# A Householder step whose norm and products come out of the strip matmuls, the masked column made by VectorE

## The chip, the cores and the metric

One NeuronCore of a Trainium2 chip runs the whole program. The metric is device time in microseconds, the median of three runs: 6160.08 us before the change (6158.68 to 6161.56).

## The reference, cut to what matters

A first layer (graph products and four small LSTMs, with a residual layer norm) is followed by a spectral graph layer that needs all eigenvectors of a 512 x 512 matrix:

```python
d_inv_sqrt = jnp.where(deg > 0, jax.lax.rsqrt(deg), 0.0)
L_norm = d_inv_sqrt[:, None] * (jnp.diag(deg) - A) * d_inv_sqrt[None, :]
_, U = jnp.linalg.eigh(L_norm)
agg = jnp.einsum('mn,bnd->bmd', U.T, features)
h = jax.nn.relu(agg @ W1 + b1)
out = jnp.einsum('nm,bmd->bnd', U, h @ W2 + b2)
```

## The kernel before

The eigenvectors come from a Householder tridiagonalization (510 steps), leaves of 16 by QR sweeps, divide and conquer, and a back transformation. The change touches the first of these. The matrix `lap` lies in four tiles of 128 rows; step k works on the T = 4 - (k+1)//128 tiles that are left, so 127, 128, 128 and 127 steps have T = 4, 3, 2, 1. The trailing matrix is updated only every 16 steps (`NB`): in between, the vectors v and w of each step go into the panel `pan`, which stands beside `lap` in `lapw`, four copies side by side so that every strip of columns has one. j = k % 16 is the place in the panel.

One step runs like this. TensorE multiplies column k (`acols`) with strips of `lapw` (L487), four strips of 32 output partitions per tile, and so gets the product with the matrix and the panel's coefficients at once; L491 fetches the panel's row k+1. While the strips run, VectorE takes the root that ScalarE made (L307), forms the pivot `pair`, the Householder vector `v` (L919) and two reciprocals (L911 to L921). When y is there it picks and reduces it (L924 to L934), builds the next column's old part `a1` (L932, L938) and the product for v'y (L940). It waits for the gate (L942), makes `pcol`, `tau_row` and the pieces of the next column, and the product for L499 (L958). L961 gives the next column `acols`; then come its norm's products (L886, L887), and with L499's sum the vector w (L966, L969), which goes into the panel. Four ones-matmuls per step carry sums over the partitions to all of them: the norm (L470), the gate (L495, prepared by GpSimd's L219 to L232), v'y (L497) and v'p (L499). ScalarE copies v and w into `swap` and `pan` (L310, L318, L319) and scales `pcol` (L321).

Each engine takes its instructions in the order written. Between them stand semaphores; `put` and `after` are VectorE's own, `link` is one with a wait at once.

## Time and profile before

| | us |
|---|---|
| median of the runs | 6160.08 |
| profiled execution | 6150.05 |
| its span | 6147.9 |
| VectorE busy | 4304.7 |
| TensorE matmul busy | 3290.3 |
| ScalarE busy | 932.4 |
| GpSimd busy | 790.6 |

The page's chain that ended last is VectorE in 53% and TensorE in 37% of the span; no engine is busy all the time. Busy shares are means over stages that differ: the steps of the change fill one stretch, and what an edit in them is worth is read from the order of time of one step.

### The profile page before, as it was taken

The numbers are of one execution on the slowest core, as the hardware profiler recorded it, in microseconds if no ns is written. First come the engines' busy times: TensorE is split into PE (matmuls) and PEld (weight loads), VectorE is DVE, ScalarE is ACT, GpSimd is POOL, SyncE is SP. The second block draws the span as 40 slices with busy tenths as digits, with TensorE's granted clock in tenths as the row PEclk, the third lists the DMA queues.
The fourth block names the chain that finished last, engine by engine and source line by source line (L and its number), as shares of the span: only waits on it lengthen the run. The fifth ranks groups of instructions, "written<-read, shape, count | busy, mean of one in ns | idle before, by whom it ended". The sixth has DMA issues, their size and how long they took to land.

```text
span 6147.9 us, 78861 instructions
## 1 busy us (share of the span) xinstructions
PE 3290.3 (54%) x19000; PEld 2342.0 (38%) x19000; DVE 4304.7 (70%) x27212; ACT 932.4 (15%) x4314; POOL 790.6 (13%) x3424
## 2 busy tenths in 40 slices
PE   7877738888888888777777730000002212230476
PEld 4333226565566666666666630000002212120243
DVE  1222286666677777888888889999968888889534
ACT  2432201111122222222222210000000000000000
POOL 0000001111111111111100014444430000000000
PEclk9988855555555555555555555555555555565578
DMA  2000000000000000000000000000000000000000
GB/s 55 0 0 0 0 0 1 1 1 1 1 1 1 1 1 1 1 1 1 1 1 1 1 1 1 1 1 1 1 1 0 0 0 0 0 0 0 0 0 27
DMA packets 20805, 17.38 MB, mean 3 GB/s; under 512 B 6544, under 2 KB 16784, under 8 KB 20368
## 3 DMA queue, kind: packets, MB, share of 16 engines
q1 hardware_dynamic: 20368, 12.65, 0.8%
q8 instruction: 141, 2.31, 0.2%
q14 instruction: 296, 2.42, 0.1%
HBM read 8.41 MB, written 4.20 MB: 2 GB/s over the span
## 4 chain that ended last, share of the span: by engine, by line
DVE 53%; PE 37%; issue 6%; ACT 2%; SPq 1%; POOL 0%; DMA 0%; DVEq 0%; ACTq 0%; POOLq 0%
PE bank L487 9%; PE bank L436 5%; PE bank L499 5%; PE bank L491 3%; DVE qp L1193 2%; PE bank L470 2%; PE bank L438 2%; DVE ycol L934 2%; DVE dif L1546 2%; PE bank L482 2%; DVE ts L966 1%; DVE qp L1183 1%; DVE tau_row L950 1%; DVE jcol L958 1%; DVE gated L948 1%
## 5 line engine op out<-in xcount | busy, mean ns | idle before, releaser
L487 PE MATMUL bank<-lapw,hid 128*32 128x160 f32 (+3 forms) x10200 | 660.3, 421 | 61.2 <-DVE lapw L907 17.8
L524 PE MATMUL bank<-diag,blk 128*128 128x32 f32 (+1 forms) x96 | 23.3, 416 | 1041.4 <-DVE diag L1310 1030.0
L487 PEld LDWEIGHTS bank<-lapw,hid 128*32 128x32 f32 x10200 | 395.1, 163 | 190.7 <-DVE lapw L969 83.0
L499 PE MATMUL bank<-xp,ones 128*128 128x1 f32 x1020 | 298.9, 362 | 277.9 <-DVE xp L958 277.9
L524 PEld LDWEIGHTS bank<-diag,blk 128*128 128x128 f32 x96 | 21.4, 327 | 1043.5 <-DVE diag L1310 1031.9
L219 POOL TENSOR_TENSOR sq<-hid,ltm 128x4 f32<-128x4 f32 (+3 forms) x510 | 101.0, 198 | 2324.3 <-DVE hid L961 2265.7
L497 PE MATMUL bank<-xp,ones 128*128 128x1 f32 x1020 | 299.0, 362 | 185.4 <-DVE xp L940 185.4
L436 PE MATMUL bank<-hid,onehot 128*128 x504 | 328.2, 769 | 120.0 <-DVE ga L736 67.2
L499 PEld LDWEIGHTS bank<-xp,ones 128*128 128x128 f32 x1020 | 255.3, 311 | 321.6 <-DVE xp L958 321.6
L497 PEld LDWEIGHTS bank<-xp,ones 128*128 128x128 f32 x1020 | 255.3, 311 | 229.1 <-DVE xp L940 229.1
L470 PE MATMUL bank<-xn,ones 128*128 128x2 f32 x1020 | 299.3, 363 | 18.5 <-DVE xn L887 17.6
L491 PEld LDWEIGHTS bank<-lapw,ident 128*128 128x128 f32 x956 | 240.3, 313 | 157.7 <-issue 157.7
L491 PE MATMUL bank<-lapw,ident 128*128 128x2 f32 (+1 forms) x956 | 292.0, 385 | 0.0
L495 PE MATMUL bank<-xn,ones 128*128 128x1 f32 x1020 | 289.1, 353 | 0.0
L495 PEld LDWEIGHTS bank<-xn,ones 128*128 128x128 f32 x1020 | 277.6, 332 | 10.6 <-issue 10.6
L318 ACT ACTIVATE swap<-vcols 128x4 f32<-128x4 f32 (+3 forms) x510 | 105.5, 207 | 1149.4 <-DVE xp L940 1149.4
L470 PEld LDWEIGHTS bank<-xn,ones 128*128 128x128 f32 x1020 | 255.4, 311 | 44.0 <-DVE xn L887 20.8
L924 DVE TENSOR_TENSOR yz<-bank,pick 128x128 f32<-128x128 f32 (+3 forms) x510 | 117.5, 230 | 205.5 <-PE bank L487 205.3
L239 POOL TENSOR_SCALAR zt<-lz,rot 32x32 f32<-32x32 f32 x540 | 194.8, 361 | 474.7 <-DVE rot L1240 425.2
L524 PE MATMUL bank<-wide,ones 128*128 128x128 f32 x80 | 18.3, 402 | 365.7 <-DVE wide L1310 365.7
L436 PEld LDWEIGHTS bank<-hid,onehot 128*128 128x128 f32 x504 | 108.7, 223 | 260.6 <-issue 252.3
L966 DVE TENSOR_SCALAR ts<-bank,tau_row 128x1 f32<-128x1 f32 x510 | 141.3, 277 | 65.1 <-PE bank L499 1.3
(729 smaller groups left out, 8493.1 us busy)
## 6 DMA issues: line engine op xcount, KB each, us to landing
out_x<-xs SPq DMA_DIRECT2D x16, 256.0 KB, 3.3
lapw<-in_adj SPq DMA_DIRECT2D x1, 1024.0 KB, 5.9
bias_rows<-in_L_gnn_bg SPq DMA_DIRECT2D x8, 64.0 KB, 5.6
hid<-lz SPq DMA_DIRECT2D x32, 1.0 KB, 1.7
bias_rows<-in_L_gnn_b SPq DMA_DIRECT2D x4, 64.0 KB, 5.7
wg<-in_L_gnn_Wg SPq DMA_DIRECT2D x2, 64.0 KB, 11.0
wg<-in_L_gnn_W SPq DMA_DIRECT2D x2, 64.0 KB, 3.6
xs<-in_x SPq DMA_DIRECT2D x1, 0.5 KB, 19.7
```

The costliest lines, as they stand in the source:

```text
L239: pool.tensor_scalar(zt[:, 0:2, :], lz[:, i:i + 2, :], rot[:, h, 0, i:i + 1], None, ALU.mult)
L436: m = pe.matmul(bank[4 * h + q][:, 0:cols_], wih_t[:, p - 1, q * P:(q + 1) * P], xt, start=True, stop=(t == 0))
L438: m = pe.matmul(bank[4 * h + q][:, 0:cols_], whh_t[:, p - 1, q * P:(q + 1) * P], state[:, h, 0:cols_], start=False, stop=True)
L470: pe.matmul(bank[0][:, 0:2], ones[:, 0:P], xn[:, 0:2], start=True, stop=True).then_inc(norm_ps, 1)
L482: pe.matmul(bank[4 + t][:, c0:], panx[:, 0, t * P:(t + 1) * P], panx[:, 1, c0:], start=True, stop=True).then_inc(update_ps, 1)
L487: m = pe.matmul(bank[1][32 * q:32 * q + 32, 0:(T + 1) * 32].rearrange("p (u i) -> p u i", i=32), acols[:, t, k:k + 1].to_broadcast([P, 32] ...
L491: pe.matmul(bank[2][:, 0:2 * j], unit(k), lapw[:, t0, N:N + 2 * j], start=True, stop=True).then_inc(rowz_ps, 1)
L495: pe.matmul(bank[4][:, 0:1], ones[:, 0:P], xn[:, 2:3], start=True, stop=True).then_inc(tail_ps, 1)
L497: pe.matmul(bank[3][:, 0:1], ones[:, 0:P], xp[:, 0:1], start=True, stop=True).then_inc(vy_ps, 1)
L499: pe.matmul(bank[2][:, 4 * NB:4 * NB + 1], ones[:, 0:P], xp[:, 1:2], start=True, stop=True).then_inc(vp_ps, 1)
L934: y = put(V.tensor_reduce(ycol[:, t0:], yz[:, t0:, 0:32 + 2 * j], AX.X, ALU.add))
L966: a = put(V.tensor_scalar(ts[:, 6:7], bank[2][:, 4 * NB:4 * NB + 1], tau_row[:, k:k + 1], tau_row[:, k:k + 1], ALU.mult, ALU.mult))
```

## The change

The step is rewritten. GpSimd writes the unit vector of row k+1 into the panel's column 2j (four copies), VectorE writes column k, masked below row k+1, into column 2j+1 (`masked`, four copies). The strips' product then holds, beside y, the pivot element and the squared norm, which VectorE copies into `al`. ScalarE takes the root, GpSimd makes five coefficients of one column, and VectorE the weights from them. y is formed with the column itself instead of v, and v is never formed in the loop; one ones-matmul of three columns (`xd`) gives all sums. The next column is `acols[k+1]`, then w for the panel, then the next masked column. The columns now lie in `vcols`, and v's pivot is added to them behind the loop, where the diagonals are put together differently too.

```diff
-        acols, gate_row = mix, vrow
+        acols = vcols
...
@@ -212,24 +213,25 @@
 
             linked = 0
             for k in range(STEPS):
...
+                t0, j = (k + 1) // P, k % NB
+                T = NT - t0
+                if k == 0:
+                    pool.wait_ge(a_ready, 1)
                 else:
...
+                    pool.wait_ge(y_done, k)
+                if j == 0 and k:
+                    pool.wait_ge(panx_ps, k // NB)
+                pool.tensor_copy(pan[:, t0:, :, j, 0], onehot[:, t0:, k + 1].unsqueeze(2).to_broadcast([P, T, 4])).then_inc(unit_ready, 1)
+                pool.wait_ge(al_ready, k + 1)
+                pool.tensor_scalar(coef[:, 0:1], al[:, 0:1], 0.0, 0.5, ALU.is_ge, ALU.subtract).then_inc(coef_ready, 1)
+                pool.tensor_scalar(coef[:, 1:2], al[:, 0:1], al[:, 0:1], al[:, 1:2], ALU.mult, ALU.add).then_inc(coef_link, 1)
+                pool.wait_ge(coef_link, linked + 1)
+                pool.wait_ge(coef_ready, 3 * k + 1)
+                pool.tensor_tensor(coef[:, 2:3], coef[:, 1:2], coef[:, 0:1], ALU.mult).then_inc(coef_ready, 1)
+                pool.tensor_scalar(coef[:, 3:4], al[:, 1:2], 1e-24, 1e37, ALU.is_le, ALU.mult).then_inc(coef_link, 1)
+                linked += 2
+                pool.wait_ge(coef_link, linked)
+                pool.tensor_tensor(coef[:, 4:5], coef[:, 3:4], coef[:, 1:2], ALU.add).then_inc(coef_ready, 1)
...
@@ -302,27 +304,28 @@
 
             for k in range(STEPS):
                 t0, j = (k + 1) // P, k % NB
...
                 if j == 0 and k:
                     act.wait_ge(panx_ps, k // NB)
                     act.activation(panx[:, 0, t0 * P:], bank[1][0:2 * NB, t0 * P:], ACT.Copy)
                     act.activation(panx[:, 1, t0 * P:], bank[2][0:2 * NB, t0 * P:], ACT.Copy).then_inc(panx_sb, 1)
                     act.wait_ge(updated, k // NB)
+                if k == 0:
+                    act.wait_ge(a_ready, 1)
                 act.activation(tz[:, t0:, 0], lap[:, t0:, k + 1], ACT.Copy).then_inc(edge_ready, 1)
...
+                act.wait_ge(am_ready, k + 1)
+                act.activation(swap[:, t0:, j, 0], pan[:, t0:, 0, j, 1], ACT.Copy).then_inc(v2_ready, 1)
+                act.wait_ge(al_ready, k + 1)
+                act.activation(root[:, 0:1], al[:, 0:1], ACT.Sqrt, scale=al[:, 0:1], bias=al[:, 1:2]).then_inc(norm_root, 1)
+                act.wait_ge(norm_root, 2 * k + 1)
+                act.wait_ge(coef_ready, 3 * k + 1)
+                act.activation(root[:, 1:2], coef[:, 0:1], ACT.Copy, scale=root[:, 0:1]).then_inc(norm_root, 1)
+                act.wait_ge(p_ready, 2 * k + 2)
+                act.activation(w0[:, t0:], pcol[:, t0:], ACT.Copy, scale=th[:, 0:1]).then_inc(w0_ready, 1)
+                act.activation(p_row[:, k:k + 1], wts[:, 0:1], ACT.Copy)
+                act.activation(tau_row[:, k:k + 1], th[:, 0:1], ACT.Copy)
+                act.wait_ge(w_ready, k + 1)
+                act.activation(swap[:, t0:, j, 1], pan[:, t0:, 0, j, 0], ACT.Copy).then_inc(w2_ready, 1)
+                act.activation(ends_row[:, k, :], bank[3][:, 0:3:2], ACT.Copy).then_inc(vy_saved, 1)
             act.activation(tz[:, NT - 1:, 0], lap[:, NT - 1:, N - 1], ACT.Copy).then_inc(edge_ready, 1)
 
             for w in range(SWEEPS):
                 t0, j = (k + 1) // P, k % NB
                 T, c0 = NT - t0, t0 * P
-                pe.wait_ge(norm_in, 2 * (k + 1))
-                pe.matmul(bank[0][:, 0:2], ones[:, 0:P], xn[:, 0:2], start=True, stop=True).then_inc(norm_ps, 1)
                 if k:
                     pe.wait_ge(w_ready, k)
-                    pe.wait_ge(v2_ready, k)
                 if j == 0 and k:
                     pe.wait_ge(w2_ready, k)
+                    pe.wait_ge(v2_ready, k)
...
                     pe.wait_ge(updated, k // NB)
+                pe.wait_ge(a_ready, k + 1)
+                pe.wait_ge(am_ready, k + 1)
+                pe.wait_ge(unit_ready, k + 1)
                 for t in range(t0, NT):
                     strips = lapw[:, t, c0:].rearrange("p (u q i) -> p u q i", q=4, i=32)
                     for q in range(4):
@@ -491,15 +495,10 @@
                     pe.matmul(bank[2][:, 0:2 * j], unit(k), lapw[:, t0, N:N + 2 * j], start=True, stop=True).then_inc(rowz_ps, 1)
                 if k:
                     pe.wait_ge(vy_saved, k)
-                pe.wait_ge(tail_in, k + 1)
-                pe.matmul(bank[4][:, 0:1], ones[:, 0:P], xn[:, 2:3], start=True, stop=True).then_inc(tail_ps, 1)
-                pe.wait_ge(x_ready, k + 1)
-                pe.matmul(bank[3][:, 0:1], ones[:, 0:P], xp[:, 0:1], start=True, stop=True).then_inc(vy_ps, 1)
-                pe.wait_ge(x2_ready, k + 1)
-                pe.matmul(bank[2][:, 4 * NB:4 * NB + 1], ones[:, 0:P], xp[:, 1:2], start=True, stop=True).then_inc(vp_ps, 1)
+                pe.wait_ge(x_ready, 2 * k + 2)
+                pe.matmul(bank[3][:, 0:3], ones[:, 0:P], xd[:], start=True, stop=True).then_inc(vy_ps, 1)
             j = STEPS % NB
             pe.wait_ge(w_ready, STEPS)
-            pe.wait_ge(v2_ready, STEPS)
             pe.matmul(bank[2][:, 0:2 * j], unit(STEPS), lapw[:, NT - 1, N:N + 2 * j], start=True, stop=True).then_inc(rowz_ps, 1)
             pe.wait_ge(diag_in, 1)
             for t in range(NT):
...
             V.memset(swap[:], 0.0)
-            V.memset(pair[:], 0.0)
-            link(V.memset(scrow[:], 0.0))
+            V.memset(p_row[:], 0.0)
+            V.memset(wts[:, 1:2], 2.0)
+            link(V.memset(wts[:, 3:4], 1.0))
...
@@ -874,22 +874,21 @@
             def after(at):
                 dve.wait_ge(tri_link, at)
 
-            bcol_ = pole_gap
-            V.tensor_copy(bcol_[:, :, 0], lap[:, :, 0])
+            V.tensor_tensor(c4[:, 8:9], lap[:, 0, 0:1], ident[:, 0:1], ALU.mult)
             V.tensor_tensor(acols[:, :, 0], lap[:, :, 0], ltm[:, :, 0], ALU.mult).then_inc(a_ready, 1)
-
-            def norms(k):
-
-                t0, e = (k + 1) // P, (k + 1) % P
-                a = acols[:, t0:, k]
-                dve.wait_ge(a_ready, k + 1)
-                V.tensor_tensor(xn[:, 1:2], acols[:, t0, k:k + 1], ident[:, e:e + 1], ALU.mult).then_inc(norm_in, 1)
-                V.tensor_tensor_reduce(jcol[:, 0, t0:], a, a, 1.0, 1e-32, ALU.mult, ALU.add, xn[:, 0:1]).then_inc(norm_in, 1)
-
-            norms(0)
             adds = 0
             rowz = 0
 
+            def masked(k):
+
+                t0 = (k + 1) // P
+                shape = [P, NT - t0, 4]
+                dve.wait_ge(a_ready, k + 1)
+                V.tensor_tensor(pan[:, t0:, :, k % NB, 1], acols[:, t0:, k].unsqueeze(2).to_broadcast(shape), ltm[:, t0:, k + 1].unsqueeze(2).to_broadcast(shape),
+                                ALU.mult).then_inc(am_ready, 1)
...
@@ -898,102 +897,110 @@
 
             for k in range(STEPS):
                 t0, j = (k + 1) // P, k % NB
...
+                T, c0, e = NT - t0, t0 * P, (k + 1) % P
+                a_, here = acols[:, t0:, k], T * 32 + 2 * j
                 if j == 0 and k:
                     for t in range(t0, NT):
                         adds += 1
                         dve.wait_ge(update_ps, adds)
                         m = V.tensor_tensor(lap[:, t, c0:], lap[:, t, c0:], bank[4 + t][:, c0:], ALU.add)
                     m.then_inc(updated, 1)
...
+                    masked(k)
 
                 dve.wait_ge(y_done, k + 1)
+                V.tensor_scalar(al[:], bank[1][:, here:here + 2], 1e-36, None, ALU.add).then_inc(al_ready, 1)
                 a = put(V.tensor_tensor(yz[:, t0:, 0:32], bank[1][:, 0:T * 32].rearrange("p (t i) -> p t i", i=32),
                                         pick[:].unsqueeze(1).to_broadcast([P, T, 32]), ALU.mult))
                 if j:
                     dve.wait_ge(w2_ready, k)
...
                     a = put(V.tensor_tensor(yz[:, t0:, 32:32 + 2 * j], panel_cols(j, t0), panel_rows(bank[1][:, T * 32:T * 32 + 32], j, T), ALU.mult))
+                after(a)
+                y = put(V.tensor_reduce(ya[:, t0:, 1], yz[:, t0:, 0:32 + 2 * j], AX.X, ALU.add))
+                dve.wait_ge(edge_ready, k + 1)
+                if j:
                     rowz += 1
                     dve.wait_ge(rowz_ps, rowz)
...
+                    after(put(V.tensor_tensor(tz[:, t0:, 1:1 + 2 * j], panel_cols(j, t0), panel_rows(bank[2], j, T), ALU.mult)))
+                a1done = put(V.tensor_reduce(ya[:, t0:, 0], tz[:, t0:, 0:1 + 2 * j], AX.X, ALU.add))
+                after(y)
+                V.tensor_tensor_reduce(jcol[:, 0, t0:], a_, ya[:, t0:, 1], 1.0, 0.0, ALU.mult, ALU.add, xd[:, 2:3]).then_inc(x_ready, 1)
+                dve.wait_ge(norm_root, 2 * k + 1)
+                r = put(V.reciprocal(ts[:, 0:1], root[:, 0:1]))
                 after(a1done)
+                V.tensor_tensor(xd[:, 0:2], ya[:, t0, :], ident[:, e:e + 1].to_broadcast([P, 2]), ALU.mult).then_inc(x_ready, 1)
+                dve.wait_ge(norm_root, 2 * k + 2)
+                dve.wait_ge(coef_ready, 3 * k + 2)
+                after(r)
+                p = put(V.tensor_scalar(wts[:, 0:1], ts[:, 0:1], coef[:, 2:3], root[:, 1:2], ALU.mult, ALU.add))
+                dve.wait_ge(coef_ready, 3 * k + 3)
+                c = put(V.reciprocal(cn_row[:, k:k + 1], coef[:, 4:5]))
+                after(p)
+                q = put(V.tensor_scalar(ts[:, 1:2], al[:, 0:1], wts[:, 0:1], coef[:, 4:5], ALU.mult, ALU.add))
+                m = put(V.tensor_tensor(yam[:, t0:, :], ya[:, t0:, :], ltm[:, t0:, k + 1].unsqueeze(2).to_broadcast([P, T, 2]), ALU.mult))
+                after(c)
+                g = put(V.tensor_tensor(wts[:, 2:5:2], wts[:, 0:1].to_broadcast([P, 2]), cn_row[:, k:k + 1].to_broadcast([P, 2]), ALU.mult))
+                after(q)
+                V.reciprocal(th[:, 0:1], ts[:, 1:2]).then_inc(p_ready, 1)
+                after(m)
                 if k:
                     dve.wait_ge(w0_ready, k)
...
+                V.scalar_tensor_tensor(pcol[:, t0:], yam[:, t0:, 0], wts[:, 0:1], yam[:, t0:, 1], ALU.mult, ALU.add).then_inc(p_ready, 1)
+                dve.wait_ge(p_ready, 2 * k + 1)
+                h = put(V.tensor_scalar(th[:, 1:2], th[:, 0:1], th[:, 0:1], wts[:, 0:1], ALU.mult, ALU.mult))
+                dve.wait_ge(p_ready, 2 * k + 2)
                 after(g)
...
+                b = put(V.scalar_tensor_tensor(nbcol[:, t0:], pcol[:, t0:], wts[:, 4:5], yam[:, t0:, 0], ALU.mult, ALU.subtract))
                 dve.wait_ge(vy_ps, k + 1)
...
+                V.tensor_tensor_reduce(jcol[:, 1, 0:2], bank[3][:, 1:3], wts[:, 3:5], 1.0, 0.0, ALU.mult, ALU.add, zy[:, 0:1])
+                z = put(V.tensor_tensor_reduce(jcol[:, 2, 0:3], bank[3][:, 0:3], wts[:, 0:3], 0.5, 0.0, ALU.mult, ALU.add, zy[:, 1:2]))
+                after(max(z, h, b))
+                x = put(V.tensor_tensor(xk[:], zy[:], th[:], ALU.mult))
+                after(x)
+                am = pan[:, t0:, 0, j, 1]
+                V.scalar_tensor_tensor(acols[:, t0:, k + 1], am, xk[:, 0:1], nbcol[:, t0:], ALU.mult, ALU.subtract).then_inc(a_ready, 1)
                 dve.wait_ge(w0_ready, k + 1)
...
+                V.scalar_tensor_tensor(pan[:, t0:, :, j, 0], am.unsqueeze(2).to_broadcast([P, T, 4]), xk[:, 1:2], w0[:, t0:].unsqueeze(2).to_broadcast([P, T, 4]),
                                        ALU.mult, ALU.subtract).then_inc(w_ready, 1)
+                if k + 1 < STEPS and (k + 1) % NB:
+                    masked(k + 1)
 
             j = STEPS % NB
             dve.wait_ge(rowz_ps, rowz + 1)
             dve.wait_ge(w2_ready, STEPS)
             dve.wait_ge(edge_ready, STEPS + 1)
             after(put(V.tensor_tensor(tz[:, NT - 1:, 1:1 + 2 * j], panel_cols(j, NT - 1), panel_rows(bank[2], j, 1), ALU.mult)))
...
+            after(put(V.tensor_reduce(ya[:, NT - 1, 0:1], tz[:, NT - 1, 0:1 + 2 * j], AX.X, ALU.add)))
+            V.tensor_tensor(c4[:, 9:10], ya[:, NT - 1, 0:1], ident[:, P - 1:P], ALU.mult)
             dve.wait_ge(a_ready, STEPS + 1)
             for t in range(NT):
...
                 lo = 1 if t == 0 else 0
                 m = V.tensor_tensor_reduce(tail[:, t * P:(t + 1) * P - lo], acols[:, t, t * P - 1 + lo:(t + 1) * P - 1], ident[:, lo:], 1.0, 0.0, ALU.mult, ALU.add, c4[:, 4 + t:5 + t])
             after(put(m))
...
+            V.memset(diag[:], 0.0)
+            for t in range(NT):
                 m = V.tensor_scalar(wide[:, t, :], ident[:], c4[:, 4 + t:5 + t], None, ALU.mult)
...
+            after(put(m))
+            V.tensor_copy(diag[:, 0, 0:1], c4[:, 8:9])
+            V.tensor_copy(diag[:, NT - 1, P - 1:P], c4[:, 9:10]).then_inc(diag_in, 1)
             dve.wait_ge(vy_saved, STEPS)
...
+            use, live_ = slice(0, STEPS), junk[:, 0:STEPS]
+            after(put(V.tensor_scalar(live_, cn_row[:, use], 1e-30, None, ALU.is_gt)))
+            after(put(V.tensor_tensor(vrow[:, use], cn_row[:, use], ends_row[:, use, 1], ALU.mult)))
             dve.wait_ge(diag_ps, 1)
             link(V.tensor_copy(diag_row[:], bank[0][:]))
             link(V.tensor_copy(off_row[:, 0:N - 1], bank[1][:, 1:N]))
...
+            link(V.tensor_tensor(tail[:, use], off_row[:, use], live_, ALU.mult))
+            link(V.tensor_tensor(off_row[:, use], off_row[:, use], tail[:, use], ALU.subtract))
+            link(V.tensor_tensor(tail[:, use], p_row[:, use], live_, ALU.mult))
+            link(V.tensor_tensor(off_row[:, use], off_row[:, use], tail[:, use], ALU.subtract))
+            link(V.tensor_scalar(live_, live_, -1.0, 1.0, ALU.mult, ALU.add))
+            link(V.tensor_tensor(tail[:, use], ends_row[:, use, 0], live_, ALU.mult))
+            link(V.tensor_tensor(diag_row[:, 1:STEPS + 1], vrow[:, use], tail[:, use], ALU.add))
+            for t in range(NT):
+                lo = 1 if t == 0 else 0
+                band = slice(t * P - 1 + lo, (t + 1) * P - 1)
+                link(V.tensor_tensor(tail[:, t * P:(t + 1) * P - lo], ident[:, lo:], p_row[:, band], ALU.mult))
+                link(V.tensor_tensor(vcols[:, t, band], vcols[:, t, band], tail[:, t * P:(t + 1) * P - lo], ALU.add))
```

## Rows read from the trace of the kernel before

**Rows 1.** Stretch table, the 510 steps: length, busy PE, PEld, DVE, ACT, POOL, clock.

```profile
889.60:3608.00 2718.40, 2149.24 (x15537) 1682.82 (x15537) 2026.60 (x15307) 608.76 (x3630) 349.56 (x1785) 0.50 0.01 1
```

**Rows 2.** Order of time, one step, three tiles: start, duration, engine, line, tiles.

```profile
2407.87 1.05 PEld L487 LDWEIGHTS bank<-lapw,hid 128*32 128x32 f32 x24 [0.18 <-DVE lapw L969]
...
2409.31 0.60 PE L491 MATMUL bank<-lapw,ident 128*128 128x12 f32 x2
2409.45 0.26 DVE L924 TENSOR_TENSOR yz<-bank,pick 128x96 f32<-128x96 f32 x1 [0.37 <-PE bank L487]
...
2411.37 0.22 DVE L957 SCALAR_TENSOR_TENSOR ats<-hid,scrow,ltm 128x3 f32<-128x3 f32 x1
2411.51 0.15 DVE L958 CUSTOM_DVE_ANT_0 jcol<-vcols,pcol 128x3 f32<-128x3 f32 x1
...
2411.63 0.23 DVE L961 SCALAR_TENSOR_TENSOR hid<-ats,bank,bm 128x3 f32<-128x3 f32 x1
...
2411.73 0.59 PE L499 MATMUL bank<-xp,ones 128*128 128x1 f32 x2 [0.54 <-DVE xp L958]
...
2411.96 0.18 DVE L886 TENSOR_TENSOR xn<-hid,ident 128x1 f32<-128x1 f32 x1
...
2412.35 0.28 DVE L966 TENSOR_SCALAR ts<-bank,tau_row 128x1 f32<-128x1 f32 x1
...
2412.66 0.24 DVE L969 SCALAR_TENSOR_TENSOR lapw<-vcols,ts,w 128x12 f32<-128x12 f32 x1
...
2412.96 1.05 PEld L487 LDWEIGHTS bank<-lapw,hid 128*32 128x32 f32 x24 [0.18 <-DVE lapw L969]
```

**Rows 3.** The same view, four tiles left.

```profile
895.35 1.80 PEld L487 LDWEIGHTS bank<-lapw,hid 128*32 128x32 f32 x32 [0.18 <-DVE lapw L969]
...
897.78 0.29 DVE L924 TENSOR_TENSOR yz<-bank,pick 128x128 f32<-128x128 f32 x1 [1.22 <-PE bank L487]
...
901.27 1.80 PEld L487 LDWEIGHTS bank<-lapw,hid 128*32 128x32 f32 x32 [0.18 <-DVE lapw L969]
```

**Rows 4.** The same view, two tiles left.

```profile
2851.53 0.52 PEld L487 LDWEIGHTS bank<-lapw,hid 128*32 128x32 f32 x16 [0.18 <-DVE lapw L969]
...
2855.88 0.52 PEld L487 LDWEIGHTS bank<-lapw,hid 128*32 128x32 f32 x16 [0.18 <-DVE lapw L969]
...
2856.68 0.50 PEld L491 LDWEIGHTS bank<-lapw,ident 128*128 128x128 f32 x2 [0.28 <-issue]
...
2857.01 0.21 DVE L924 TENSOR_TENSOR yz<-bank,pick 128x64 f32<-128x64 f32 x1
```

**Rows 5.** The same view, one tile left.

```profile
3562.54 0.20 PEld L487 LDWEIGHTS bank<-lapw,hid 128*32 128x32 f32 x8 [0.18 <-DVE lapw L969]
...
3562.91 0.50 PEld L491 LDWEIGHTS bank<-lapw,ident 128*128 128x128 f32 x2 [0.17 <-issue]
...
3563.66 0.17 DVE L924 TENSOR_TENSOR yz<-bank,pick 128x32 f32<-128x32 f32 x1
...
3566.72 0.20 PEld L487 LDWEIGHTS bank<-lapw,hid 128*32 128x32 f32 x8 [0.18 <-DVE lapw L969]
```

**Rows 6.** Groups by line: count, busy us, mean ns, idle time before them.

```profile
L239 POOL TENSOR_SCALAR zt<-lz,rot 32x32 f32<-32x32 f32 x540 | 194.8, 361 | 474.7 <-DVE rot L1240 425.2
...
L321 ACT ACTIVATE w<-pcol,tau_row 128x4 f32<-128x4 f32 (+3 forms) x510 | 150.9, 296 | 114.6 <-DVE tau_row L950 114.6
...
L232 POOL TENSOR_TENSOR xn<-sq 128x1 f32<-128x1 f32 x383 | 74.9, 195 | 30.0
...
L1087 DVE TENSOR_SCALAR lq<-lq 32x1 f32<-32x1 f32 x36 | 8.7, 242 | 0.0
```

**Rows 7.** Order of time again, start of a panel's transposes, four tiles.

```profile
986.75 0.20 ACT L310 ACTIVATE swap<-lapw 128x4 f32<-128x4 f32 x1
987.07 0.10 PEld L477 LDWEIGHTS bank<-ident,lapw 128*32 128x32 f32 x1 [0.51 <-DVE lapw L969]
```

**Rows 8.** Order of time, a wide link behind the last step.

```profile
3618.95 0.69 DVE L994 TENSOR_TENSOR junk<-pair,vrow 128x510 f32<-128x510 f32 x1
```

102 lines of the change are left out of this document (8 added, 94 removed).

## The prediction

> **What bounds the kernel now.** I read the stretch table first: the 510 Householder steps that the change rewrites fill 889.6 to 3608 us, 2718.4 of the 6147.9 us span, with TensorE at clock 0.50, its 1.2 GHz level, all the time [rows 1]. Nothing outside is touched but a short stretch behind it. Then the order of time of one step with three tiles left (T = 3) [rows 2]. It repeats every 2412.96 - 2407.87 = 5.09 us: the strip products of `lapw` take 1.58 us until VectorE starts `yz`, then VectorE works almost without a gap from 2409.45 to its product for the last ones-matmul (L958), that matmul ends at 2412.32, and two more VectorE instructions (to 2412.90) release the next strips. So a step is a loop of latencies: strips, VectorE's chain, one small matmul, VectorE again. With four tiles the loop is 901.27 - 895.35 = 5.92 us, 2.43 of it strips [rows 3]. With two it is 4.35 and with one 4.18 [rows 4, 5]. There the strips are done sooner (0.94 and 0.51 us: start of the small matmul behind them plus the 0.14 seen in rows 2), but `yz` starts only 1.12 us after them with one tile (3563.66 - 3562.54): the root and the vector `v` are still being made on VectorE. This hidden chain ends last only for T = 2 and 1.
>
> **What the change removes.** Three of the four ones-matmuls per step, with their round trips; one stays. The norm now comes out of the strips themselves: column 2j of the panel holds the unit vector, column 2j+1 the masked column, so `bank[1]` delivers alpha and the squared norm together with y. The chain that made `v` before `yz` goes, which for T = 1 uncovers 1.12 - 0.51 = 0.61 us and for T = 2, where `yz` starts 1.13 after the strips [rows 4], 0.19 us. What comes instead stands behind the strips: root, coefficients and weights can only start after them.
>
> **How I price a VectorE chain.** From rows 2: an instruction that waits for nothing starts its predecessor's duration less 0.08 after it (L957 0.22, L958 0.14 later); one that needs a result starts 0.04 after that ends (L957 to L961, L966 to L969). One that stands behind two waits, the second being the late one, starts 0.10 after (L961 ends 2411.86, L886 at 2411.96). Work on a few columns costs 0.15 (L958) to 0.18 (L886), I take 0.16; with one per-partition scalar 0.22 (L957). With two it costs 0.24 on 32 partitions [rows 6] and 0.28 with an operand from PSUM (L966); I take 0.25 for the three in SBUF.
>
> **The new step, T = 3, j = 6, from the moment y is there.** `al` 0.00; `yz` 0.07; its panel part 0.24 to 0.43; reduction 0.47 to 0.75; `tz` product 0.67 to 0.86 (the row product in `bank[2]` is there by 0.50, L491 starts 0.14 before `yz` and lasts 0.60); second reduction 0.90 to 1.09; the products for `xd` 1.01 to 1.33, a reciprocal between them; `wts` 1.35 to 1.60 (behind a third wait, 0.10). Then the reciprocal of `coef[4]`, which comes from GpSimd (below), `ts[1]` 1.67 to 1.92, `yam` 1.84, `g` 1.92, `th` 2.00 to 2.17, `pcol` 2.08 to 2.30, `h` 2.22 to 2.47, `nbcol` 2.39 to 2.61, the two `zy` sums 2.53 to 2.77, `xk` 2.81 to 2.97, new column 3.01 to 3.24, `w` for the panel 3.16 to 3.40, masked column 3.32 to 3.49. The one matmul (1.33 + 0.05 + 0.60 + 0.03 = 2.01) is hidden behind this. ScalarE's root and its product (0.15 + 0.03 + 0.38, then 0.05 + 0.29; 0.29 is L321 with one operand as scale [rows 6], the root has a second, for which I add 0.09) end at 0.90 and are hidden too.
>
> **The masked column.** It is a 128 x 4T product, about 0.17 us by L958's and L886's size, and it is the last thing that the strips wait for: they need `w_ready`, `a_ready`, `am_ready` and `unit_ready`, four waits where there were two. It starts 0.16 after `w` and so adds 0.09 to the chain. Between VectorE and TensorE one late wait costs 0.06 (L969 to L487 [rows 2]); with three awaited, the late one second, 0.12 (ScalarE ends 986.95, TensorE starts 987.07 [rows 7]). Four I put at 0.145, bounds 0.06 and 0.20. Behind these waits in TensorE's queue stands the whole step. The unit columns come from GpSimd, which is free for them after about 1.6 us; hidden by 1.8 us of slack. In 31 steps (every sixteenth) it goes behind the update of `lapw` instead; there it is not in front of the panel's transposes but in front of the strips all the same, so these steps pay about what the others pay.
>
> **GpSimd's chain.** Five one-column instructions: two with immediates, one with two pointer scalars, two tensor products. The product costs 0.195, the tensor-scalar form 0.361 with one pointer and 32 elements [rows 6], and the dependent product starts 0.08 after its producer (L232's idle 30.0 us by 383). No row shows the one-column forms. Bounds: each as a product, 0.20, or as the row, 0.33 and 0.45 for two pointers. I take 0.22 and 0.38, nearer the product, as 32 elements are part of the 0.361. From `al` at 0.15: 0.08 + 0.19 + 0.38 + 0.08 + 0.165 + 0.22 + 0.08 + 0.195 + 0.05 = 1.44, ready at 1.59. VectorE could take it at 1.52 for T = 3 and at 1.30 for T = 1, so from T = 3 down it sets the time, by 0.03 to 0.25 us.
>
> **The sum.** Chain 3.49 + 0.145 + strips 1.58 = 5.21 for T = 3, against 5.09: +0.12. By the same steps T = 4 (j = 1): 6.06 against 5.92, +0.14. T = 2: 3.63 + 0.94 = 4.57 against 4.35, +0.22; T = 1: 3.63 + 0.51 = 4.14 against 4.18, -0.04. There are 127, 128, 128 and 127 such steps: 17.8 + 15.4 + 28.2 - 5.1 = +56 us. The same bookkeeping gives the old step some 0.02 more than its rows show; I take off 510 x 0.02 = 10. Behind the steps: wide links 0.72 each [rows 8], seven where three were, and eight of 128 columns at about 0.32, less eight of 128 columns at about 0.2: +4. Together +50 on a profiled execution of 6150.05 us, which lies 10 us under the median of the runs, 6160.08. Forecast: 6210 us.
>
> **Rivals.** *GpSimd is dear* (0.16): its tensor-scalar forms cost 0.33 and 0.45, the coefficients are ready at 1.88, and each step grows by 0.3 to 0.5, with one tile by 0.2: over the j by average +179, less the 10, plus the 4, 6333 us (6260 to 6345). For it: the only row of that form, 0.361. Against: its 32 elements and its pointer. The Trainium skill's GPSIMD Engine Reference, section Engine selection, says to leave elementwise work to VectorE, GpSimd being some two times slower for two inputs; here the one-column product is 0.195 against VectorE's 0.15 to 0.18, so the trace shows less, but the hops of 0.08 come on top, and five instructions in a row are where that rule would bite.
>
> *Faster* (0.28): the hand-overs cost what single waits cost, 0.06 before the strips and 0.04 before `wts`, and GpSimd's forms cost 0.20. Then the GpSimd chain is ready at 1.37 and hidden for T = 4 to 2, and the steps are: first the cheap GpSimd, 5 us over before by the average over j; less 510 x 0.09 = 46; less 255 x 0.06 = 15; less the 10; plus 4: -62, 6100 us. It decides if the strips start under 0.08 after the masked column and `coef` is there before VectorE asks. T = 1 gains 0.3 to 0.4 per step in it, which is where the old hidden chain is uncovered [rows 5]. Half of it (one of the two cheap) gives 6140.
>
> *Nothing measurable* (0.12): the pieces cancel, within 12 us, about 0.2%, which is what a measurement of this kernel can tell from no change. The change doing something other than it says isn't open: the masked column is made by VectorE, and ScalarE's copy of `v` (L319) goes; in the kernel before GpSimd made no such column, so what is timed is the whole new step.
>
> *Shared reads*, inside the forecast's range: L886 took 0.18 while a GpSimd product ran beside it, L958 0.15 [rows 2]. The Trainium skill (SBUF — State Buffer, Who interferes with whom) says that a VectorE instruction with two SBUF inputs contends with a GpSimd instruction that reads SBUF. Four such fall beside GpSimd's new chain; at 0.02 each that would be +20 to +40 us, 6240 us.
>
> **How the numbers follow.** Forecast 6210 (6175 to 6255, the bounds of the waits before the strips and half of those of GpSimd's forms), 0.44; dear GpSimd 0.16; faster 0.28; same 0.12. Slower by over 0.2%: 0.60. The range leaves about one in ten on each side: 6110 to 6300.
>
> **What would show it.** In the new profile: T = 3 steps of 5.2 us between strips, T = 1 of 4.1; masked column 0.17 and the strips 0.14 behind its end; idle VectorE time before the reciprocal of `coef`, released by GpSimd, growing from T = 3 to T = 1; no idle time released by the one matmul or by the root. I am wrong if that idle time is missing, if GpSimd's tensor-scalar takes 0.3 or more, or if T = 2 comes out under 4.35.

## The result and the profile after

The changed kernel takes 6290.24 us (median of 4 runs, 6286.64 to 6292.10) against 6159.38 for the kernel before on the same chip: 1.0213 times as long, 95% interval 1.0195 to 1.0231, +131 us. The forecast was 6210, +50. The sign was right, but the loss is more than twice the forecast's: the time lies outside the 6175 to 6255 that were given with it, inside the outer bounds of 6110 to 6300, and within the 6260 to 6345 of the rival *dear GpSimd*. The profiled execution took 6289.45 us, with a span of 6287.7 us.

Two parts of its page, busy time and the chain that ended last:

```profile
PE 2491.2 (40%) x15940; PEld 1659.8 (26%) x15940; DVE 3972.7 (63%) x25687; ACT 1179.3 (19%) x5334; POOL 1117.7 (18%) x4699
DVE 51%; PE 29%; issue 10%; POOL 8%; ACT 2%; SPq 1%; DVEq 0%; DMA 0%; ACTq 0%; POOLq 0%
```

The stretch of the 510 steps, as in [rows 1] (length, busy PE, PEld, DVE, ACT, POOL, clock):

```profile
892.67:3743.77 2851.10, 1347.70 (x12480) 997.92 (x12480) 1690.77 (x13768) 854.15 (x4646) 676.33 (x3061) 0.50 0.00 1
```

It is 2851.1 us long where it was 2718.4: +132.7. The span grew by 139.8, of which 3.1 lies ahead of the steps and 4.0 behind them. Nearly all that is to be explained is in the steps, and the clock is the same. TensorE is busy 802 us less and VectorE 336 us less, and yet the stretch is longer. So busy time was not what set it.

The step that answers to [rows 2] (three tiles, step 246, j = 6), in order of time:

```profile
2488.43 0.16 DVE L911 TENSOR_SCALAR al<-bank 128x2 f32<-128x2 f32 x1 [1.82 <-PE bank L491]
...
2488.68 0.23 POOL L226 TENSOR_SCALAR coef<-al 128x1 f32<-128x1 f32 x1 [3.80 <-DVE al L911]
...
2488.89 0.35 POOL L227 TENSOR_SCALAR coef<-al 128x1 f32<-128x1 f32 x1
...
2489.32 0.19 POOL L230 TENSOR_TENSOR coef<-coef 128x1 f32<-128x1 f32 x1
...
2489.59 0.23 POOL L231 TENSOR_SCALAR coef<-al 128x1 f32<-128x1 f32 x1
...
2489.79 0.27 DVE L934 TENSOR_SCALAR wts<-ts,coef,root 128x1 f32<-128x1 f32 x1
...
2489.91 0.19 POOL L234 TENSOR_TENSOR coef<-coef 128x1 f32<-128x1 f32 x1
...
2490.14 0.16 DVE L936 RECIPROCAL cn_row<-coef 128x1 f32<-128x1 f32 x1
...
2491.52 0.23 DVE L960 SCALAR_TENSOR_TENSOR vcols<-lapw,xk,nbcol 128x3 f32<-128x3 f32 x1
2491.66 0.23 DVE L962 SCALAR_TENSOR_TENSOR lapw<-lapw,xk,w 128x12 f32<-128x12 f32 x1
2491.80 0.17 DVE L887 TENSOR_TENSOR lapw<-vcols,ltm 128x12 f32<-128x12 f32 x1
...
2492.20 1.08 PEld L491 LDWEIGHTS bank<-lapw,vcols 128*32 128x32 f32 x24 [1.87 <-DVE lapw L962]
2492.23 1.51 PE L491 MATMUL bank<-lapw,vcols 128*32 128x128 f32 x24 [1.81 <-DVE lapw L887]
...
2493.80 0.16 DVE L911 TENSOR_SCALAR al<-bank 128x2 f32<-128x2 f32 x1 [1.82 <-PE bank L491]
```

Two places stand out. The reciprocal L936 starts 0.03 behind the end of GpSimd's last sum L234 (2490.105 to 2490.139). The masked column ends at 2491.97, the strips' weights load starts at 2492.20 and their first product at 2492.23, 0.26 behind it. In [rows 2] the same passage took 0.06 (L969 ends 2412.90, L487 starts 2412.96).

The same steps as in [rows 3 to 5] in the changed kernel, four tiles, then two, then one:

```profile
901.42 0.16 DVE L911 TENSOR_SCALAR al<-bank 128x2 f32<-128x2 f32 x1 [2.67 <-PE bank L491]
```

```profile
2966.49 0.16 DVE L911 TENSOR_SCALAR al<-bank 128x2 f32<-128x2 f32 x1 [1.18 <-PE bank L491]
...
2968.21 0.16 DVE L936 RECIPROCAL cn_row<-coef 128x1 f32<-128x1 f32 x1 [0.20 <-POOL coef L234]
...
2971.21 0.16 DVE L911 TENSOR_SCALAR al<-bank 128x2 f32<-128x2 f32 x1 [1.18 <-PE bank L491]
```

```profile
3699.00 0.16 DVE L911 TENSOR_SCALAR al<-bank 128x2 f32<-128x2 f32 x1 [0.76 <-PE bank L491]
...
3700.71 0.16 DVE L936 RECIPROCAL cn_row<-coef 128x1 f32<-128x1 f32 x1 [0.22 <-POOL coef L234]
...
3703.27 0.16 DVE L911 TENSOR_SCALAR al<-bank 128x2 f32<-128x2 f32 x1 [0.76 <-PE bank L491]
```

Step by step (the next `al` after the first of these is at 907.66):

| tiles | before | forecast | measured | over the forecast |
|---|---|---|---|---|
| 4 | 5.92 | 6.06 | 6.24 | 0.18 |
| 3 | 5.09 | 5.21 | 5.37 | 0.16 |
| 2 | 4.35 | 4.57 | 4.72 | 0.15 |
| 1 | 4.18 | 4.14 | 4.27 | 0.13 |

The excess changes by 0.05 only while the strips shrink from 2.4 to 0.5 us. Most of it sits in a fixed part of the step, not in the strips or the panel.

Groups by line, the new small ones, as [rows 6]:

```profile
L227 POOL TENSOR_SCALAR coef<-al 128x1 f32<-128x1 f32 x510 | 177.1, 347 | 0.0
L934 DVE TENSOR_SCALAR wts<-ts,coef,root 128x1 f32<-128x1 f32 x510 | 139.3, 273 | 47.0 <-POOL coef L230 8.6 <-POOL coef L234 0.9 <-DVE ts L928 0.6
...
L226 POOL TENSOR_SCALAR coef<-al 128x1 f32<-128x1 f32 x510 | 118.6, 233 | 1935.4 <-DVE al L911 1935.4
...
L887 DVE TENSOR_TENSOR lapw<-vcols,ltm 128x16 f32<-128x16 f32 (+3 forms) x510 | 86.5, 170 | 0.0
L936 DVE RECIPROCAL cn_row<-coef 128x1 f32<-128x1 f32 x510 | 82.8, 162 | 56.4 <-POOL coef L234 39.6
```

And what one line of TensorE's queue left, the wait for the masked column (count, ns):

```profile
L486 PEldq EVENT_SEMAPHORE  x509: 51/51/51, 898.8 to 3741.2; - x170
```

The durations came out as priced: 0.23 and 0.35 for GpSimd's forms (0.22 and 0.38 forecast), 0.170 for the masked column (0.17). The last row is the clue to the passage. Of TensorE's four waits ahead of the strips, the one written first in the code (for `w`) rides on the load; the others are two instructions of their own in front of it. In step 246 the trace has the one for the masked column, written third, at 2492.015, 0.04 behind its end, the other (for the column, written second, and the unit, written fourth, both long fulfilled) at 2492.126, and the load at 2492.202. So the records do not keep the written order, except that the first rides on the load.

So two theories: **A**, the late wait stands as an instruction of its own with another behind it, and that costs 0.08 to 0.17 us a step; **C**, GpSimd's chain holds VectorE's reciprocal (the recorded texts of the runs on GpSimd's chain call this their Theory A). Their rival: VectorE's own order sets the step and both only seem late.

### The profile page after: what moved, and what is told of

Read it like the earlier page. It is cut to its first block, busy times and chain, and to the rows that moved or that the text cites. A ratio compares the mean times of both kernels' runs of the same rounds, so it can differ in the third digit from the quotient of the medians.

```text
span 6287.7 us, 73604 instructions
## 1 busy us (share of the span) xinstructions
PE 2491.2 (40%) x15940; PEld 1659.8 (26%) x15940; DVE 3972.7 (63%) x25687; ACT 1179.3 (19%) x5334; POOL 1117.7 (18%) x4699
## 4 chain that ended last, share of the span: by engine, by line
DVE 51%; PE 29%; issue 10%; POOL 8%; ACT 2%; SPq 1%; DVEq 0%; DMA 0%; ACTq 0%; POOLq 0%
PE bank L491 11%; PE bank L439 5%; POOL coef L227 2%; PE bank L441 2%; DVE qp L1200 2%; DVE vcols L960 2%; DVE dif L1553 2%; DVE nbcol L952 2%; PE bank L483 2%; DVE ts L938 2%; POOL coef L231 1%; POOL coef L226 1%; DVE xk L957 1%; DVE al L911 1%; DVE qp L1190 1%
## 5 line engine op out<-in xcount | busy, mean ns | idle before, releaser
L491 PE MATMUL bank<-lapw,vcols 128*32 128x160 f32 (+3 forms) x10200 | 659.8, 419 | 934.4 <-DVE lapw L887 922.0
L491 PEld LDWEIGHTS bank<-lapw,vcols 128*32 128x32 f32 x10200 | 439.1, 162 | 1021.2 <-DVE lapw L962 922.9
L499 PE MATMUL bank<-xd,ones 128*128 128x3 f32 x1020 | 285.5, 350 | 500.3 <-DVE xd L930 500.3
L226 POOL TENSOR_SCALAR coef<-al 128x1 f32<-128x1 f32 x510 | 118.6, 233 | 1935.4 <-DVE al L911 1935.4
L499 PEld LDWEIGHTS bank<-xd,ones 128*128 128x128 f32 x1020 | 256.0, 312 | 550.0 <-issue 548.3
L318 ACT ACTIVATE root<-al 128x1 f32<-128x1 f32 x510 | 198.3, 389 | 718.4 <-DVE al L911 718.4
L323 ACT ACTIVATE w<-pcol,th 128x4 f32<-128x4 f32 (+3 forms) x510 | 151.7, 297 | 790.4 <-DVE pcol L947 790.4
L227 POOL TENSOR_SCALAR coef<-al 128x1 f32<-128x1 f32 x510 | 177.1, 347 | 0.0
L934 DVE TENSOR_SCALAR wts<-ts,coef,root 128x1 f32<-128x1 f32 x510 | 139.3, 273 | 47.0 <-POOL coef L230 8.6
L321 ACT ACTIVATE root<-coef,root 128x1 f32<-128x1 f32 x510 | 151.0, 296 | 16.7
L918 DVE TENSOR_REDUCE ya<-yz 128x4 f32<-128x128 f32 (+7 forms) x510 | 140.4, 275 | 17.5
```

The costliest lines, as they stand in the source:

```text
L226: pool.tensor_scalar(coef[:, 0:1], al[:, 0:1], 0.0, 0.5, ALU.is_ge, ALU.subtract).then_inc(coef_ready, 1)
L227: pool.tensor_scalar(coef[:, 1:2], al[:, 0:1], al[:, 0:1], al[:, 1:2], ALU.mult, ALU.add).then_inc(coef_link, 1)
L318: act.activation(root[:, 0:1], al[:, 0:1], ACT.Sqrt, scale=al[:, 0:1], bias=al[:, 1:2]).then_inc(norm_root, 1)
L321: act.activation(root[:, 1:2], coef[:, 0:1], ACT.Copy, scale=root[:, 0:1]).then_inc(norm_root, 1)
L323: act.activation(w0[:, t0:], pcol[:, t0:], ACT.Copy, scale=th[:, 0:1]).then_inc(w0_ready, 1)
L491: m = pe.matmul(bank[1][32 * q:32 * q + 32, 0:(T + 1) * 32].rearrange("p (u i) -> p u i", i=32), acols[:, t, k:k + 1].to_broadcast([P, 32] ...
```

## The experiments

Each ratio below is to the kernel before on the same chip. The runs were made on several chips, so the difference between two of them is best taken from their ratios. Offsets given as "at 1.73" are averages over the steps of three tiles, from the start of `al`.

**The masked column's wait first**

```
-                if k:
-                    pe.wait_ge(w_ready, k)
                 if j == 0 and k:
+                    pe.wait_ge(w_ready, k)
...
-                pe.wait_ge(a_ready, k + 1)
                 pe.wait_ge(am_ready, k + 1)
+                if j:
+                    pe.wait_ge(w_ready, k)
+                pe.wait_ge(a_ready, k + 1)
                 pe.wait_ge(unit_ready, k + 1)
```

> The changed kernel with the order of TensorE's waits for the strips alone changed: the wait for the masked column comes first in the code and so rides on the instruction itself; the wait for the w half, for the column and for the unit's space come behind it as separate wait instructions. Theory A (the late wait stands as a separate wait instruction, and the passage from the masked column's end to the strips costs 0.22 to 0.23 us a step where a single attached wait costs about 0.055 to 0.14 elsewhere in the trace): the passage falls to 0.06 to 0.15, so 0.08 to 0.17 us less in each of some 500 steps, 40 to 85 us less than the changed kernel's 6290, that is 6205 to 6250. Rival B (the passage is VectorE's write of four copies becoming visible, or the weights' load itself): nothing moves, 6285 to 6295.

6191.07 us, ratio 1.0054 (1.0037 to 1.0071): 99 us gone, more than A's upper end. Step 246:

```profile
2445.52 0.17 DVE L888 TENSOR_TENSOR lapw<-vcols,ltm 128x12 f32<-128x12 f32 x1
2445.75 1.05 PEld L492 LDWEIGHTS bank<-lapw,vcols 128*32 128x32 f32 x24 [1.70 <-DVE lapw L888]
2445.75 1.51 PE L492 MATMUL bank<-lapw,vcols 128*32 128x128 f32 x24 [1.61 <-DVE lapw L888]
```

The first product starts 0.06 behind the masked column instead of 0.26, and all else in the step keeps its distances. A holds. It was under-priced because I took the passage to the load, and the first product lags the load by another 0.03 where a late separate wait stands ahead of the load (here 0.00).

**The same wait made late in the kernel before**

```
                 if k:
-                    pe.wait_ge(w_ready, k)
                     pe.wait_ge(v2_ready, k)
+                    pe.wait_ge(w_ready, k)
```

> The kernel before, with the order of two of TensorE's waits ahead of the strips exchanged: the wait for ScalarE's v half (long fulfilled) comes first in the code and rides on the instruction, the wait for w, which ends last, becomes a separate wait instruction in front of it. Nothing is computed otherwise. Theory A (a late wait as a separate instruction costs by itself, whatever the kernel: the run with the masked column's wait first gave back 0.19 us a step by its trace, from two separate instructions in a row, and a separate one is followed by the next 0.10 later and by the load another 0.08 later): one separate instruction costs 0.05 to 0.10 us a step, 25 to 50 us in all, 6185 to 6210. Rival B (what the changed kernel lost there was particular to the masked column, VectorE's last write before the strips): 6155 to 6162.

6188.34 us, ratio 1.0046 (1.0029 to 1.0063): +28 us, in A's range; the steps' stretch grew by 34 us in the trace. A holds in a kernel without any masked column of VectorE's. Its order of time, three tiles, and below it the same of the kernel before:

```profile
2410.29 0.24 DVE L969 SCALAR_TENSOR_TENSOR lapw<-vcols,ts,w 128x12 f32<-128x12 f32 x1
2410.64 1.08 PEld L487 LDWEIGHTS bank<-lapw,hid 128*32 128x32 f32 x24 [0.24 <-issue]
2410.67 1.29 PE L487 MATMUL bank<-lapw,hid 128*32 128x128 f32 x20 [0.18 <-DVE lapw L969]
```

```profile
2412.96 0.87 PE L487 MATMUL bank<-lapw,hid 128*32 128x128 f32 x12
```

The first product comes 0.14 behind `w` (2410.53 to 2410.67) where it was 0.06. Steps grew by 0.09 with four, three and two tiles and not at all with one (4.219 to 4.224). So one separate wait costs 0.09, two in a row 0.19 to 0.21 (from the run above, by stretch). With one tile the hidden chain named in the prediction covers it; with two tiles, where the prediction had it end last too, it does not.

**GpSimd's forms in another order**

```
+                pool.tensor_scalar(coef[:, 1:2], ...).then_inc(coef_link, 1)
                 pool.tensor_scalar(coef[:, 0:1], ...).then_inc(coef_ready, 1)
-                pool.tensor_scalar(coef[:, 1:2], ...).then_inc(coef_link, 1)
+                pool.tensor_scalar(coef[:, 3:4], ...).then_inc(coef_link, 1)
...
                 pool.tensor_tensor(coef[:, 2:3], ...).then_inc(coef_ready, 1)
-                pool.tensor_scalar(coef[:, 3:4], ...).then_inc(coef_link, 1)
```

> The changed kernel with GpSimd's four forms on the first two values in another order: the two-pointer form first, then the two forms with plain numbers, then the product and the quotient's factor. Theory A (GpSimd's chain to the last coefficient ends the wait of VectorE's reciprocal, 0.16 us later than forecast, because a form started behind a wait no longer overlaps the one before it): the last coefficient comes 0.2 to 0.35 us sooner after the two values, the wait is then ended by ScalarE's root or the weights, and a step loses 0.08 to 0.15 us in the stretches of T=4 and T=3 and up to 0.2 in T=1: 6215 to 6250. Rival B (VectorE's own order of instructions is what runs a step and GpSimd only seems late): 6280 to 6295.

The two waits ahead of the product are exchanged too.

6350.29 us, ratio 1.0315 (1.0298 to 1.0333): some 60 us slower than the changed kernel, in neither expected range. I missed two things, both in this step:

```profile
2507.55 0.34 POOL L226 TENSOR_SCALAR coef<-al 128x1 f32<-128x1 f32 x1 [3.98 <-DVE al L911]
...
2507.97 0.23 POOL L227 TENSOR_SCALAR coef<-al 128x1 f32<-128x1 f32 x1
...
2508.27 0.25 POOL L228 TENSOR_SCALAR coef<-al 128x1 f32<-128x1 f32 x1
...
2508.60 0.19 POOL L231 TENSOR_TENSOR coef<-coef 128x1 f32<-128x1 f32 x1
...
2508.88 0.27 DVE L934 TENSOR_SCALAR wts<-ts,coef,root 128x1 f32<-128x1 f32 x1 [0.32 <-POOL coef L231]
```

First, a form with plain numbers starts 0.08 behind the end of what stands before it (2507.97 after 2507.89, 2508.27 after 2508.20). Only the two-pointer form overlaps its predecessor, by 0.02 (2488.89 against 2488.91 in the changed kernel's step). Second, the product now comes later, and VectorE's weight waits for it (idle 0.32). GpSimd does set the step, but through whichever of its two outputs is late.

**The form on the second value at the head of the four**, on top of the better wait order

```
                 pool.wait_ge(al_ready, k + 1)
+                pool.tensor_scalar(coef[:, 3:4], al[:, 1:2], 1e-24, 1e37, ...).then_inc(coef_link, 1)
...
                 pool.tensor_tensor(coef[:, 2:3], ...).then_inc(coef_ready, 1)
-                pool.tensor_scalar(coef[:, 3:4], al[:, 1:2], 1e-24, 1e37, ...).then_inc(coef_link, 1)
```

> The changed kernel with TensorE's waits in the better order (the masked column's first), and GpSimd's form on the second value alone moved to the head of its four, so that the sum follows the product directly. Compared with the run that has the better wait order alone (6191). Theory A (the last coefficient ends the wait of VectorE's reciprocal, 0.14 us a step; the form in the tail of GpSimd's chain costs it 0.28 from the product's start to the form's and 0.32 on to the sum's): the sum starts 0.15 after the product instead of 0.60, the coefficient is there before the weight, the reciprocal starts 0.19 after the weight's start instead of 0.33, while the product itself comes 0.2 later, which the weight just allows for at T=4, 3 and 2 and which costs it up to 0.15 at T=1, where the reciprocal gains 0.28 by the same move: 0.10 to 0.14 a step, 50 to 70 us, 6120 to 6140. Rival B (VectorE's order alone sets the step): 6185 to 6195. Rival C (the product 0.2 later delays the weight by as much as the reciprocal gains, as in the run with GpSimd's other order): 6180 to 6230.

6205.43 us, ratio 1.0067 (1.0050 to 1.0084), 8 us above the wait order alone, with overlapping intervals: rival C of that text, by its mechanism. The sum does follow the product by 0.15, but the head costs 0.32 and not 0.21, for the reason just seen. The weight starts at 1.51 instead of 1.40, and so the reciprocal gains only 0.03 (1.70 against 1.73) and the instruction behind it nothing (1.82 against 1.81).

**Without GpSimd's last two operations**, same wait order

```
-                pool.tensor_scalar(coef[:, 3:4], al[:, 1:2], 1e-24, 1e37, ...).then_inc(coef_link, 1)
...
-                pool.tensor_tensor(coef[:, 4:5], coef[:, 3:4], coef[:, 1:2], ALU.add).then_inc(coef_ready, 1)
...
-                c = put(V.reciprocal(cn_row[:, k:k + 1], coef[:, 4:5]))
+                c = put(V.reciprocal(cn_row[:, k:k + 1], coef[:, 1:2]))
```

> The changed kernel with TensorE's waits in the better order, and without GpSimd's last two operations: the sum of squares itself goes to the reciprocal in place of the coefficient that has the large number added for a column that is nearly zero (so that guard is left out of the computation). Compared with the run that has the better wait order alone (6191). Theory A (the tail of GpSimd's chain is what VectorE waits for, 0.14 us at T=4, 3 and 2 and 0.28 at T=1): 70 to 90 us less, 6100 to 6120. Rival B (GpSimd only seems late): 6185 to 6195.

This kernel leaves out the guard for a column that is nearly zero. 6124.11 us, ratio 0.9936 (0.9919 to 0.9952), 73 us under the wait order alone, as expected (70 to 90). The reciprocal starts at 1.59, 0.19 behind the weight. It has lost its own wait by the edit, but that is not what frees it: in the mended kernels at the end it keeps the wait and starts at the same distance, 0.19 to 0.20. With three tiles a step is 0.09 shorter (5.217 to 5.126), with one 0.22 (4.104 to 3.883). C holds.

With the reciprocal at 1.59, which is where the prediction had it, the masked column ends at 3.495 on average with three tiles, the prediction's own figure: VectorE's chain behind the reciprocal was priced rightly.

**The reciprocal's wait first on VectorE**, ahead of the weight L934, same wait order on TensorE

```
+                after(r)
                 dve.wait_ge(norm_root, 2 * k + 2)
                 dve.wait_ge(coef_ready, 3 * k + 2)
-                after(r)
```

> The changed kernel with TensorE's waits in the better order, and of VectorE's three waits ahead of the weight the one for its own reciprocal (the last to come) put first, so that it rides on the instruction. Compared with the run that has the better wait order alone (6191). Theory A (a late separate wait costs on VectorE too): the weight starts 0.04 to 0.06 us earlier, but the reciprocal behind it waits for GpSimd's last coefficient in any case, so that the end of the step does not move: 6185 to 6193. Rival B (the weight's start is what counts, and the reciprocal follows it at a fixed distance): 20 to 30 us less, 6160 to 6172.

6184.50 us, ratio 1.0039 (1.0025 to 1.0053); it and the wait order alone overlap in their intervals, so no gain is shown by the times. The weight starts 0.08 earlier (1.32), the reciprocal does not (1.72): GpSimd holds it, as expected. With four tiles, where the chain is longer, the step gains 0.05.

**The masked column ahead of `w`**

```
+                if k + 1 < STEPS and (k + 1) % NB:
+                    masked(k + 1)
                 dve.wait_ge(w0_ready, k + 1)
                 V.scalar_tensor_tensor(pan[:, t0:, :, j, 0], ...).then_inc(w_ready, 1)
-                if k + 1 < STEPS and (k + 1) % NB:
-                    masked(k + 1)
```

> The changed kernel with VectorE's last two instructions of a step exchanged: the masked column first, w behind it. TensorE's strips need both, so the sum of work ahead of them stays; what changes is which wait is the last one: the wait for w rides on the instruction, the one for the masked column is separate. Theory A (the separate late wait costs): the passage to the strips is 0.06 to 0.10 us shorter, 30 to 50 us in all, 6240 to 6260. But w's own wait for GpSimd's partial sum now lies behind the masked column and so is covered a little better (up to 0.03 a step, 10 us more). Rival B (the passage is the same for any last write): 6275 to 6295.

6284.14 us, ratio 1.0207 (1.0190 to 1.0224), 4 us less where A expected 30 to 50 less; the time is in rival B's range. What was wrong is where the masked column can start: it needs the new column, and even ahead of `w` it starts only 0.26 behind that one's start (2487.25 against 2486.99), and ends 0.01 sooner than in the changed kernel. Its two separate waits then run their 0.23 as before, and `w`'s attached wait is over by then. The passage hangs on when the separately awaited write ends, not on which write is last.

**The masked column made by GpSimd**, as its head's first step, with the changed kernel's wait order and with the better one

```
                 pool.tensor_copy(...).then_inc(unit_ready, 1)
+                pool.wait_ge(a_ready, k + 1)
+                pool.tensor_tensor(pan[:, t0:, :, j, 1], acols[:, t0:, k]..., ltm[:, t0:, k + 1]..., ALU.mult).then_inc(am_ready, 1)
                 pool.wait_ge(al_ready, k + 1)
```

> The changed kernel with the masked column for the panel's slot made by GpSimd at the head of its step, ahead of its coefficients, as the kernel before has it for its own product, instead of by VectorE at the end of the step before. VectorE loses 0.17 us from its chain behind w, GpSimd gains a product of 0.2 to 0.3 us with its wait and puts its coefficients off if the two values are there by then. Theory A (the masked column starts when the new column ends, beside w, so it is ready 0.25 to 0.30 us after the new column where VectorE's is ready 0.5 after it): TensorE then waits for whichever of w and the masked column is later, w ends 0.17 earlier than VectorE's masked column, so the gain is at most 0.17 and probably 0.05 to 0.12 a step, 25 to 60 us less, 6230 to 6265. Rival B (GpSimd is dear for it: passage from VectorE to it 0.1, product 0.3 to 0.4 with the four copies, passage to TensorE 0.1): 0.05 to 0.15 a step more, 6315 to 6365.

> The masked column made by GpSimd as in the earlier run of that, and TensorE's wait for it first, so riding on the instruction: the two places of the masked column compared where no late separate wait stands before the strips. Theory: GpSimd's masked column ends 0.08 to 0.09 us after VectorE's would (0.30 after the new column's end instead of 0.22 to 0.24), as with the other wait order: 0.07 a step, some 30 to 35 us more than the run with VectorE's masked column and the same order (ratio 1.0054), 6215 to 6235. Rival (the difference measured before came from the late separate wait behind GpSimd's signal): equal to it, 6185 to 6200.

6321.07 us, ratio 1.0267 (1.0250 to 1.0284), against 1.0213; and 6217.87 us, ratio 1.0099 (1.0082 to 1.0116), against 1.0054. Both put GpSimd's masked column some 30 us behind VectorE's: in the first run rival B came, not A's gain, in the second the theory. The first:

```profile
2507.21 0.22 DVE L961 SCALAR_TENSOR_TENSOR vcols<-lapw,xk,nbcol 128x3 f32<-128x3 f32 x1
2507.35 0.23 DVE L963 SCALAR_TENSOR_TENSOR lapw<-lapw,xk,w 128x12 f32<-128x12 f32 x1
2507.52 0.21 POOL L227 TENSOR_TENSOR lapw<-vcols,ltm 128x12 f32<-128x12 f32 x1 [1.58 <-DVE vcols L961]
```

It starts beside `w`, 0.09 behind the new column's end, and is ready 0.52 behind its start, where VectorE's is at 0.45 (2491.97 less 2491.52). That is 0.07 a step. In the 31 steps where the panel is closed it gains instead, 0.26 each, as in the code it does not stand behind VectorE's update there. So of the two places for the masked column, VectorE's is the better by 30 us. The loss lies elsewhere.

**The mend: ScalarE makes the product**, alone and with both wait orders

```
-                pool.tensor_scalar(coef[:, 1:2], ...).then_inc(coef_link, 1)
-                pool.wait_ge(coef_link, linked + 1)
-                pool.wait_ge(coef_ready, 3 * k + 1)
-                pool.tensor_tensor(coef[:, 2:3], coef[:, 1:2], coef[:, 0:1], ALU.mult).then_inc(coef_ready, 1)
+                pool.tensor_scalar(coef[:, 1:2], ...).then_inc(coef_ready, 1)
...
+                act.wait_ge(coef_ready, 3 * k + 2)
+                act.activation(coef[:, 2:3], coef[:, 1:2], ACT.Copy, scale=coef[:, 0:1]).then_inc(norm_root, 1)
```

> The changed kernel with ScalarE making GpSimd's product, and nothing of the wait order ahead of the strips changed: what the coefficient's part of the unforeseen time is worth by itself. Theory: the weight keeps its start at 1.40 (T=3), the reciprocal starts at 1.59 instead of 1.73, at T=1 at 1.48 instead of 1.72; 0.14 us a step at T=4, 3 and 2 and 0.2 to 0.25 at T=1, 70 to 85 us less than the changed kernel, 6205 to 6225, ratio 1.008 to 1.011. Rival (the two unforeseen terms aren't a plain sum: with the passage unmended the gain is taken up by another wait): 6250 to 6290.

> The candidate: the changed kernel with TensorE's wait for the masked column first, VectorE's wait for its own reciprocal first ahead of the weight, and GpSimd's product made by ScalarE instead (a copy with a scale taken from the other value, the form ScalarE's second root has; one more instruction on ScalarE, idle there until the next term), so that GpSimd's form on the second value follows its sum of squares without the product and its wait between them. Theory (GpSimd's coefficient is what VectorE's reciprocal waits for once the passage is mended): the form starts 0.42 after the sum of squares' start instead of 0.71, the last coefficient is there at 1.39 after the two values instead of 1.68, the weight starts at 1.32 (T=3), the reciprocal at 1.51 instead of 1.73: 0.20 us a step at T=4, 3 and 2 and 0.25 at T=1, some 100 to 115 us under the run with the wait order alone (ratio to the kernel before 1.0054), 6075 to 6095, ratio about 0.988. Rival (the product comes later from ScalarE than from GpSimd and holds the weight up): the weight at 1.45 to 1.5, 30 to 60 us less only, 6130 to 6160, ratio 0.996 to 1.000.

ScalarE's signal now stands for the product too, so that VectorE has two waits ahead of the weight instead of three.

Alone: 6214.39 us, ratio 1.0093 (1.0076 to 1.0109), 74 us less than the changed kernel, as expected. The reciprocal starts at 1.57 (1.59 expected), the weight at 1.37, 0.03 sooner than before. With both wait orders: **6098.64 us, ratio 0.9902 (0.9885 to 0.9918)**, some 60 us faster than the kernel before and 190 faster than the changed one. The candidate's step:

```profile
2405.59 0.16 DVE L912 TENSOR_SCALAR al<-bank 128x2 f32<-128x2 f32 x1 [1.63 <-PE bank L492]
...
2406.43 0.29 ACT L321 ACTIVATE coef<-coef 128x1 f32<-128x1 f32 x1
2406.47 0.23 POOL L228 TENSOR_SCALAR coef<-al 128x1 f32<-128x1 f32 x1
...
2406.79 0.19 POOL L232 TENSOR_TENSOR coef<-coef 128x1 f32<-128x1 f32 x1
2406.86 0.27 DVE L934 TENSOR_SCALAR wts<-ts,coef,root 128x1 f32<-128x1 f32 x1
...
2407.05 0.15 DVE L936 RECIPROCAL cn_row<-coef 128x1 f32<-128x1 f32 x1
```

The sum is done at 2406.98, before VectorE asks for it, and the reciprocal starts 1.45 after `al` instead of 1.71 in this step (1.51 instead of 1.73 on average). The three mends one by one are worth 99, 74 and 9 us (the last not clear of noise), 182 together; the measured 190 says that they nearly add up. The candidate missed its expected upper end by 4 us.

## Why the prediction was right in sign and wrong in size

- **What bounds the step** (latencies, not busy time): right. TensorE lost 37% of its busy time in the steps and the stretch grew.
- **The masked column** (0.17, last before the strips, 0.09 added to the chain): 0.17 measured, ready where it was put but for 0.05 (3.54 after `al`, 3.49 forecast).
- **The waits ahead of the strips**, put at 0.145 with bounds 0.06 and 0.20: this step failed. It is 0.23 to the load and 0.26 to the first product. I scaled from [rows 7] by the number of waits. There the late wait is written third, not second, and the three waits left one separate instruction before the load (at 986.993, load 0.12 behind ScalarE's end); what counted in the runs is whether the late one is written first (0.06, [rows 2]) and how many separate ones stand in the queue from it on. 0.085 there and 0.02 from load to `al`: 0.105 x 510 = 54 us of the excess.
- **GpSimd's chain**, ready at 1.59: the durations were right (0.23 and 0.35, forecast 0.22 and 0.38), one term of the sum was not, the second that failed. I let the form L231 start 0.165 after the product; it starts 0.27 after it, 0.08 behind its end. The reciprocal started at 1.71 or 1.72 in the steps of three, two and one tile, 0.12 late. The rest of VectorE's chain then took 0.07 less than forecast with three tiles; 0.04 of it is that L938 starts 0.08 after L936 here, where it starts 0.12 after it in the run without GpSimd's last two operations. By the table less the 0.105, what is left of both is 0.075, 0.055, 0.045 and 0.025 us from four tiles down to one: 25 us.
- **The old step's 0.02**, taken off as 10 us: nothing of it shows; this is what the sum leaves, no run prices it. 54 + 25 + 10 = 89, and the steps' excess is 132.7 - 46 = 87 us.
- **The shape of the idle time**: right. It appears before L936, released by GpSimd, 0.07 with three tiles in step 246, 0.20 and 0.22 with two and one. No idle time was released by the one matmul or by the root. Of the signs of being wrong, "GpSimd's tensor-scalar takes 0.3 or more" was written loosely: the two-pointer form takes 0.35, but the sum had 0.38 for it, and the plain one takes 0.23.
- **T = 1 shorter** (4.14): wrong, 4.27. The uncovered 0.61 us was eaten by the same two terms; in the candidate it is 3.85.
- **Behind the steps** +4: measured +4.0.
- **Rivals.** The time lies in the range of *dear GpSimd*, but by luck: the forms cost 0.23 and 0.35, not 0.33 and 0.45, and more than half of the excess came from the waits. Its chain was dearer than forecast only by an overlap that failed. The Trainium skill's GPSIMD Engine Reference, Engine selection, has it some two times slower for elementwise work on two inputs; the masked product took 0.214 on GpSimd against VectorE's 0.170, 1.26 times, and the kernel with it was 30 us slower. *Faster* named its deciding points rightly (the strips under 0.08 behind the masked column, `coef` there before VectorE asks): the candidate has both, at 0.05 and 2406.98 against 2407.05, and gained 60 us, as that rival's 6100 had it. That the times agree to 2 us is partly luck: its GpSimd forms were to cost 0.20, while the candidate has the coefficient ready in time with forms of 0.23 and 0.35, as the product is gone from the chain. *Shared reads* show nothing: VectorE's product L930, with two SBUF inputs, runs beside GpSimd's L231 in step 246 and takes 0.142 on average, and 0.141 in the run without L231; the two-scalar form L934 takes 0.273 in both.

What stays open: why a separate wait followed by a second one takes 0.11 to it and 0.08 to the load was measured, not explained. No run has the late wait second or fourth of the four, where it would stand in the last separate instruction; and none priced the first-product lag of 0.03 by itself.

## What to carry to other kernels

Where an instruction has several waits, write first the one that is fulfilled last; the others, fulfilled earlier, showed no cost then, while a late one behind it cost 0.09 to 0.2 us each time in these runs. In a loop of latencies, price each engine hand-over by the row whose waits have the same order, and draw the small engine's chain instruction by instruction, with its gaps, before putting a step on it. A small product may be cheaper on an engine that idles than where its inputs are made, if a chain behind it is what others wait for.

## What the runs showed of the hardware that was not expected

- TensorE: from the end of the last written operand to the first strip product 0.06 with the late wait on the load itself, 0.14 with it as one separate instruction, 0.26 with a second separate one behind it (changed kernel; 0.06 and 0.14 from the runs with the masked column's wait first and with the late wait in the kernel before). VectorE has the same in small: 0.08 between the weight's start with the late wait first and third.
- GpSimd on one column: a tensor-scalar form with plain numbers (0.23) starts 0.08 behind the end of each predecessor that the runs show (another such form, the two-pointer form, a product), waited for or not; a form with two pointers (0.35) starts 0.02 ahead of its predecessor's end, and a product that waits for nothing new 0.05 ahead of it (2508.74 after one from 2508.60 to 2508.79).
- ScalarE's root with two per-partition operands takes 0.389 us on one column, a copy with one 0.296. No row of the kernel before had the root in this form; the forecast's 0.38 and 0.29 were right.
